# A transformer kernel on one core: score masks and norm scales moved from one engine to another

## The reference

```
for l in range(4):                                   # H = 16 heads of width 16
    h = rmsnorm(x, n1[l])
    q, k, v = split(h @ Wqkv[l].T + bqkv[l], 3)
    q, k = apply_rope(q), apply_rope(k)
    x = x + merge(sdpa(q, k, v, causal_bias)) @ Wo[l].T + bo[l]
    h2 = rmsnorm(x, n2[l])
    qc = h2 @ Wq_c[l].T
    kc, vc = split(memory @ Wkv_c[l].T, 2)
    x = x + merge(sdpa(qc, kc, vc, cross_bias)) @ Wo_c[l].T
    h3 = rmsnorm(x, n3[l])
    x = x + silu(h3 @ Wg[l].T) * (h3 @ Wu[l].T) @ Wd[l].T
# rmsnorm(x, w) = x * rsqrt(mean(x*x, -1) + eps) * w
# sdpa: softmax(q @ k.T * scale + bias) @ v; a bias is 0 where a key is allowed and -1e30 elsewhere
```

## Time and profile before

| what | value |
|---|---|
| median of 3 runs | 621.46 us (620.04 to 621.73) |
| span of the profiled execution | 617.9 us |
| TensorE busy | 564.1 us (91%) |
| weight loads busy (beside TensorE) | 421.8 us (68%) |
| VectorE busy | 353.5 us (57%) |
| ScalarE busy | 279.5 us (45%) |
| GpSimd busy | 117.7 us (19%) |
| instructions | 13676 |

### The profile page before, as it was taken

One profiled execution on the slowest core, in us unless ns is written; L12 is line 12 of the kernel. 1 busy time (PEld: TensorE's weight loads), 2 busy tenths in 40 slices (PEclk: granted clock), 3 DMA queues, 4 the chain that ended last, 5 costly groups with the idle time before them and its releaser, 6 DMA issues.

```text
span 617.9 us, 13676 instructions
## 1 busy us (share of the span) xinstructions
PE 564.1 (91%) x5806; PEld 421.8 (68%) x5806; DVE 353.5 (57%) x680; ACT 279.5 (45%) x490; POOL 117.7 (19%) x124
## 2 busy tenths in 40 slices
PE   4989998999999899999998989999898989999855
PEld 1666655988767566988766658987666558897523
DVE  5896445466564454674554455574554364752787
ACT  0254444633355336433544446342554547445523
POOL 4252100012323100020612000122312001252110
PEclk9999999999999999999999999999999999999969
DMA  8800020010500200201400200204000200000001
GB/s 334 345 2 25 12 69 2 5 65 1 205 2 4 102 1 3 68 1 27 180 1 36 70 2 2 69 1 189 16 2 1 71 0 2 0 1 2 2 1 39
DMA packets 4676, 30.29 MB, mean 49 GB/s; under 512 B 1153, under 2 KB 1665, under 8 KB 2818
## 3 DMA queue, kind: packets, MB, share of 16 engines
q1 hardware_dynamic: 4610, 29.35, 12.5%
HBM read 28.82 MB, written 0.52 MB: 47 GB/s over the span
## 4 chain that ended last, share of the span: by engine, by line
PE 77%; DVE 10%; ACT 8%; issue 3%; POOL 1%; DMA 1%; SPq 0%; DVEq 0%; POOLq 0%
PE psD L326 18%; PE QD L621 12%; PE psD L634 9%; PE QD L408 6%; PE QD L443 4%; ACT PTR L1253 3%; PE psD L320 3%; PE QD L436 3%; PE QD L394 3%; DVE AQ L1803 3%; PE psD L463 2%; PE QD L431 2%; PE psD L359 2%; PE psD L484 2%; PE psD L470 2%
## 5 line engine op out<-in xcount | busy, mean ns | idle before, releaser
L1253 ACT ACTIVATE PTR<-QD 128x2048 f32<-128x2048 f32 x40 | 75.1, 1878 | 41.8 <-PE QD L443 21.5
L326 PE MATMUL psD<-WAB,hT 128*128 128x256 f32 (+1 forms) x216 | 70.1, 465 | 2.2 <-DVE hT L1744 2.2
L2492 POOL TENSOR_TENSOR rstd<-ms,mhalf 128x2 f32<-128x2 f32 x26 | 19.9, 764 | 271.8 <-DVE ms L1729 270.6
L1803 DVE TENSOR_REDUCE AQ<-QD 128x8 f32<-128x2048 f32 (+1 forms) x24 | 55.0, 2290 | 27.0 <-PE QD L408 27.0
L621 PE MATMUL QD<-HH,WFH 128*128 128x256 f32 x224 | 67.4, 301 | 0.4 <-DVE WFL L1903 0.4
L1903 DVE TENSOR_TENSOR WFL<-WC,WFH 128x512 fp32r<-128x512 f32 x64 | 48.0, 755 | 32.2 <-ACT WFH L1297 32.1
L621 PE MATMUL QD<-HL,WFH 128*128 128x256 f32 x224 | 63.3, 283 | 0.0
L621 PE MATMUL QD<-HH,WFL 128*128 128x256 f32 x224 | 63.3, 283 | 0.0
L1800 DVE TENSOR_REDUCE AQ<-QD 128x16 f32<-128x2048 f32 x16 | 36.7, 2293 | 39.9 <-PE QD L408 39.9
L634 PE MATMUL psD<-WC,HID 128*128 128x256 f32 x256 | 58.2, 380 | 0.0
L326 PEld LDWEIGHTS psD<-WAB,hT 128*128 128x128 f32 x216 | 39.7, 195 | 21.0 <-issue 14.2
(11 more groups left out here) (172 smaller groups left out, 1021.2 us busy)
## 6 DMA issues: line engine op xcount, KB each, us to landing
WC<-in_wc SPq DMA_DIRECT2D x4, 3072.0 KB, 10.9
WAB<-in_wa SPq DMA_DIRECT2D x4, 1024.0 KB, 4.9
WAB<-in_wb SPq DMA_DIRECT2D x4, 1024.0 KB, 4.7
WF<-in_wf SPq DMA_DIRECT2D x1, 3072.0 KB, 22.8
bias<-in_bias SPq DMA_DIRECT2D x4, 512.0 KB, 3.4
WAB<-in_wt SPq DMA_DIRECT2D x1, 1024.0 KB, 6.0
X<-in_x SPq DMA_DIRECT2D x2, 256.0 KB, 2.8
out_x<-X SPq DMA_DIRECT2D x4, 128.0 KB, 2.4
```

The costliest lines, as they stand in the source:

```text
L326: mm = pe.matmul(bank(l, use)[:, col:col + n], lhs(k), rhs(k), start=(k == 0), stop=(k == KT - 1))
L1253: nc.scalar.activation(PTR[:, r % 2, :], QD[:, :], ACT.Exp, scale=SCALE).then_inc(t_exp, 1)
L1803: v = dve.tensor_reduce(QKR[b][:, t, 0, h, MAXROW].rearrange("p (s r) -> p r s", r=SG_H), QD[:, :].rearrange("p (r s n) -> p r s n", r=4, ...
```

## The change

Three things, and an order to go with them.

Scores: `scores` no longer writes the masks, and its matmuls start the bank afresh. `maxima` goes through the banks head by head: one `tensor_tensor_reduce` each, which multiplies nothing, adds the mask to the scores in place (`ALU.add`, scaled by -1) and keeps the running minimum, which goes to the head's own column of `MAXROW`. `causB` is now 256 wide, 0 in its left half and the causal mask in its right half. `QD` is read and written in place by these instructions.

Norms 0 and 1: `norm_T` transposes `X` itself and waits only for the residual; the scale rstd is multiplied in behind the projections, in `biased_qk`, `biased_v` and `cross_q`, where each row has its own partition again. `normalise` is left for i = 2 only. `add_bo` on GpSimd, which changes X, now waits until the transposes and the squares have read it.

Orders: the lists of calls of all engines are written in another order throughout.

```diff
@@ norm_T
-                pe.wait_ge(h_set[b], l * NORMS + i + 1)
-                transposes(l, f"n{i}{b}", hs[:, 2 * b:2 * b + 2, :])
+                if i == 2:
+                    pe.wait_ge(h_set[b], l + 1)
+                elif i == 1:
+                    pe.wait_ge(*emptied(l, f"wo{b}"))
+                elif l == 0:
+                    pe.wait_ge(x_set[b], 1)
+                else:
+                    pe.wait_ge(*emptied(l - 1, f"y{b}"))
+                transposes(l, f"n{i}{b}", (hs if i == 2 else X)[:, 2 * b:2 * b + 2, :])
@@ scores
-                    pe.wait_ge(mask_set, 1)
...
-                for a in range(4):
-                    if cross:
-                        pe.matmul(quad[a].rearrange("p (s n) -> p s n", s=2), identB[:, :],
-                                  maskB[:, 2 * b:2 * b + 2, :].rearrange("p t n -> p (t n)").unsqueeze(1).broadcast_to([P, 2, L]),
-                                  start=True, stop=False, skip_group_check=True)
...
-                                           QKT[b][rows(a), s, L:L + keys], start=False, stop=True, skip_group_check=True)
+                                           QKT[b][rows(a), s, L:L + keys], start=(at == 0), stop=True, skip_group_check=True)
@@ biased_qk
-                dve.tensor_tensor(QK[b][:, t, :], bank(l, use)[:, :], bias[:, 0:2 * D], ALU.add).then_inc(free(l, use), 1)
+                dve.scalar_tensor_tensor(QK[b][:, t, :], bank(l, use)[:, :], rstd[:, b, t:t + 1], bias[:, 0:2 * D], ALU.mult, ALU.add)\
+                   .then_inc(free(l, use), 1)
@@ maxima
                 if cross:
-                    v = dve.tensor_reduce(QKR[b][:, :, 0, h, MAXROW].rearrange("p t (s r) -> p r s t", r=SG_H),
-                                          QD[:, :].rearrange("p (r s t n) -> p r s t n", r=4, s=2, t=QT), AX_X, ALU.max, negate=True)
+                    if l == 0:
+                        dve.wait_ge(mask_set, 1)
+                    for a in range(4):
+                        for n, s in enumerate(ss):
+                            for q in range(QT):
+                                v = dve.tensor_tensor_reduce(quad[a][:, (2 * n + q) * P:(2 * n + q + 1) * P],
+                                                             quad[a][:, (2 * n + q) * P:(2 * n + q + 1) * P], maskB[:, 2 * b + q, :],
+                                                             -1.0, NO_MAX, ALU.add, ALU.min,
+                                                             accum_out=QKR[b][:, q, 0, SG_H * s + a, MAXROW:MAXROW + 1])
                 else:
-                    v = dve.tensor_reduce(QKR[b][:, t, 0, h, MAXROW].rearrange("p (s r) -> p r s", r=SG_H),
-                                          QD[:, :].rearrange("p (r s n) -> p r s n", r=4, s=len(ss)), AX_X, ALU.max, negate=True)
+                    keys = (t + 1) * P
+                    for a in range(4):
+                        for n, s in enumerate(ss):
+                            v = dve.tensor_tensor_reduce(quad[a][:, n * keys:(n + 1) * keys], quad[a][:, n * keys:(n + 1) * keys], causB[:, L - keys:L],
+                                                         -1.0, NO_MAX, ALU.add, ALU.min,
+                                                         accum_out=QKR[b][:, t, 0, SG_H * s + a, MAXROW:MAXROW + 1])
@@ cross_q
+                dve.wait_ge(rstd_set[b], l * NORMS + 2)
+                for t in range(QT):
+                    v = dve.tensor_scalar(QKR[b][:, t, 0, :, 0:HD], bank(l, use)[:, t * D:(t + 1) * D].rearrange("p (h d) -> p h d", h=H),
+                                          rstd[:, B + b, t:t + 1], None, ALU.mult)
@@ layer, TensorE (two of many lines)
+                scores(l, 8)
+                cross_qT(l, 1, 1)
                 outputs_T(l, 6)
-                scores(l, 8)
```

More of the change, by code:

```diff
@@ L922, in _ @@
             cross_kv(0, 0)
+            norm_T(0, 1, 0)
             pv(0, 3)
             scores_T(0, 4)
+            cross_kT(0, 0)
             maxima_T(0, 5)
+            cross_q(0, 0)
+            scores_T(0, 5)
+            cross_qT(0, 0, 0)
+            cross_qT(0, 0, 1)
             outputs_T(0, 3)
-            norm_T(0, 1, 0)
-            cross_kT(0, 0)
-            scores_T(0, 5)
-            cross_q(0, 0)
             pv(0, 4)
-            cross_qT(0, 0, 0)
+            scores(0, 6)
             outputs_T(0, 4)
-            cross_qT(0, 0, 1)
-            scores(0, 6)
             pv(0, 5)
@@ L1069, in rest @@
                 cross_kT(NL - 1, 1)
+                cross_qT(NL - 1, 1, 0)
                 pv(NL - 1, 6)
-                cross_qT(NL - 1, 1, 0)
+                scores(NL - 1, 8)
                 outputs_T(NL - 1, 6)
-                scores(NL - 1, 8)
                 pv(NL - 1, 7)
@@ L1112, in rest @@
                 gate_up(NL - 1, 1, 5)
+                down(NL - 1, 1, range(0, 4))
                 gate_up(NL - 1, 1, 6)
                 gate_up(NL - 1, 1, 7)
-                down(NL - 1, 1, range(0, 4))
                 window_T(0)
@@ L1839, in cross_q @@
                 no_maxima(b)
-                dve.tensor_copy(QKR[b][:, :, 0, :, 0:HD], bank(l, use)[:, :].rearrange("p (t h d) -> p t h d", t=QT, h=H))\
-                   .then_inc(free(l, use), 1)
+                dve.wait_ge(rstd_set[b], l * NORMS + 2)
+                for t in range(QT):
+                    v = dve.tensor_scalar(QKR[b][:, t, 0, :, 0:HD], bank(l, use)[:, t * D:(t + 1) * D].rearrange("p (h d) -> p h d", h=H),
+                                          rstd[:, B + b, t:t + 1], None, ALU.mult)
+                v.then_inc(free(l, use), 1)
             def cross_kv(l, b):
@@ L2089, in layer @@
                 residual(l - 1, 1, "y1")
+                biased_v(l, 0)
+                weigh_T(l, 0, 1)
                 mean_square(l, 0, 1)
-                normalise(l, 0, 1)
-                weigh_T(l, 0, 1)
-                biased_v(l, 0)
                 maxima(l, 2)
@@ L2106, in layer @@
                 maxima(l, 4)
+                cross_kv(l, 0)
                 residual(l, 0, "wo0")
-                cross_kv(l, 0)
+                maxima(l, 5)
+                split_low(l, 0)
+                weigh_T(l, 1, 0)
                 mean_square(l, 1, 0)
-                maxima(l, 5)
-                normalise(l, 1, 0)
-                weigh_T(l, 1, 0)
+                cross_q(l, 0)
                 divide(l, 3)
-                cross_q(l, 0)
                 maxima(l, 6)
@@ L2232, in _ @@
             maxima(0, 4)
+            mask_by_key()
             residual(0, 0, "wo0")
+            maxima(0, 5)
             mean_square(0, 1, 0)
-            maxima(0, 5)
-            normalise(0, 1, 0)
             cross_kv(0, 0)
@@ L2242, in rest @@
                 weigh_T(0, 1, 0)
+                cross_q(0, 0)
                 divide(0, 3)
-                cross_q(0, 0)
+                maxima(0, 6)
                 divide(0, 4)
-                maxima(0, 6)
                 divide(0, 5)
@@ L2251, in rest @@
                 split_low(0, 0)
+                split_low(0, 1)
+                weigh_T(0, 1, 1)
                 mean_square(0, 1, 1)
-                normalise(0, 1, 1)
-                weigh_T(0, 1, 1)
                 cross_q(0, 1)
-                split_low(0, 1)
+                maxima(0, 8)
                 divide(0, 6)
-                maxima(0, 8)
                 divide(0, 7)
@@ L2325, in rest @@
                 residual(NL - 2, 1, "y1")
+                biased_v(NL - 1, 0)
+                weigh_T(NL - 1, 0, 1)
                 mean_square(NL - 1, 0, 1)
-                normalise(NL - 1, 0, 1)
-                weigh_T(NL - 1, 0, 1)
-                biased_v(NL - 1, 0)
                 maxima(NL - 1, 2)
```

562 lines of the change are left out of this document (276 added, 286 removed).

## The result

The changed kernel takes 631.77 us (median of 4 runs, 630.66 to 632.27), the kernel before 620.75 beside it: ratio 1.0174 [1.0159, 1.019], so 11 us slower. I had forecast slower, which it is, but by 30.5 us. The profiled execution has a span of 630.5 us, 12.6 more than before.

What follows compares the result with a forecast made beforehand. TensorE, busy 96% of a layer, was taken as the bound, with a chain through QD's one set of banks hidden. Sum: 617.9 - 31.4 + 62 + 4 - 4 = 648.5 us span, so 652 us; range 603 to 703.

Steps and rivals of the forecast that it cites:

- masks off TensorE: By-query scores: removing their mask matmuls saves 7.9 us a layer, 31.4 us in all, without cover.
- norms, and the orders: Norms 0 and 1: transposes of X no longer wait for the normalised rows, and the start gets shorter: -4 us.
- maxima by masked pairs, with the queue on VectorE: Longer maxima stick out 15.6 us a layer, +62 us; VectorE work queued behind them adds +4.
- the cover of a round: Time from a reduce's start to TensorE's next use of QD, new order included: 2.25 to 4.25 us, 31 a layer.
- I take 0.25 + 0.07 = 0.32 and 0.38 + 0.07 = 0.45: VectorE's price in us of a pair over 128 and 256 columns, 0.07 for writing the result; maxima last 5.1 or 3.6.
- The stretch of gate_up and the quantised stage at the end stay as they are: End of the program: a sign of being right, that these parts do not change.
- the same 3.6 outside it: The median of the runs, 621.46 us, lies 3.6 us above the profiled span; added to the predicted span.
- C: Rival on the maxima: pair price just at the crossing, TensorE's waits equal its savings, 620 to 623 us; chance 0.06.
- the crossing: Pair price below which the change gains: about 0.27 and 0.40 us, where 8 us a layer stick out.
- A: Rival on the maxima: cheap pairs, 0.19 and 0.34 us, nearly all covered, 593 us; chance 0.18 for 593 to 619.
- B: Rival on the maxima: pairs at full cost, 0.48 and 0.61 us, 36 us a layer stick out, 735 us; chance 0.14.
- the waits on QD: Sign in TensorE's wait list: maxima of QD on top with some 60 us, in 30 or more places.

Runs made afterwards that it cites:

- o_plain: The kernel before, its orders and norms kept, with one reduce per round over scores that carry no mask: 593.46 us, 0.9553.
- n_plain: The changed kernel with one reduce per round over scores that carry no mask, new orders and norms kept: 596.42 us, 0.9609.
- o_masks: The kernel before with only the score masks moved to VectorE's pairs, norms and orders as before: 641.53 us, 1.0347.
- n_slow: The changed kernel with an unused 0.8 us VectorE reduce over constants ahead of every maximum: 661.9 us, 1.0639.
- n_cross: The changed kernel with self rounds masked on TensorE and one reduce each, only cross rounds masked by VectorE: 627.93 us, 1.0125.
- o_norms: The kernel before with only the two norms' scale moved behind the projections, masks and orders as before: 620.9 us, 1.0001.
- t_old: The changed kernel with before's order on four engines from the middle of the last layer's second feed-forward half to the end: 622.76 us, 1.005.
- n_warm: The changed kernel with dummy transposes on TensorE where it would wait ahead of the scores or the maxima's transposes: 632.33 us, 1.0191.

## Why the prediction was right or wrong

The 631.8 us lie inside the wide range of 603 to 703, and just below the forecast's own 634 to 684; the loss is a third of what was forecast. The spans 617.9 (before), 591.2 (o_plain), 594.6 (n_plain) and 630.5 (after) give each term of my sum its measured size:

| term | forecast | measured |
|---|---|---|
| masks off TensorE | -31.4 | -26.7 |
| norms, and the orders | -4 | +3.4 |
| maxima by masked pairs, with the queue on VectorE | +62 + 4 | +35.9 |
| sum | +30.6 | +12.6 |

**The maxima: right mechanism, wrong price.** This is the term that failed. The claim that the maxima on the one set of QD's banks become the wait, and that the cover of a round is 2.3 to 4.3 us, holds: o_masks, n_plain and n_slow show it. The step at fault is "I take 0.25 + 0.07 = 0.32 and 0.38 + 0.07 = 0.45". The first part was right to the hundredth, with some luck: the operations last 327 and 458 ns and not 291 and 424, but they overlap by 0.08 us and not by the 0.04 that I took from L1744 in the earlier trace rows, whose instructions come in twos, so that the 0.44 us are the mean of 0.40 and 0.48. The 0.07 us for the accumulator's result was not there: the read runs beside the next pair. The earlier trace rows had shown this on ScalarE (the next activation starts before the read ends), and I added 0.07 all the same. With 0.25 and 0.38, 4.25 and 3.35 us are needed, and against the same ten covers 0, 0, 0.35, 0.75, 0.75, 1.1, 1.45, 1.25, 1.45 and 1.25 us stick out: 8.4 us a layer, for which n_plain against after shows 7.7, 8.8 and 8.2. An error of 0.07 us in the pair was one of 7 us in a layer, because behind the cover every nanosecond of a pair counts 16 or 8 times a round.

The Trainium skill's 120 + columns cycles ("VectorE: DVE Perf Modes", section on the TRN2 errata), which I had put aside because the durations in the earlier trace rows were longer, give an estimate of 0.26 and 0.39 us, and the pairs follow each other at 0.25 and 0.38. In this trace the figure fits the pitch (start of one to start of the next), and not the duration of 327 and 458 ns. That an operation which writes out its accumulator is two instructions, as the same page of the Trainium skill says ("Two Vector instructions with no wait between them"), is what this trace shows; I had read it as speaking against the change, and the second instruction shows no cost here.

**Layer 0.** There 12.1 us stick out, not 8.4. I had scaled a steady layer by four. n_cross shows that it is the self rounds. That VectorE has the feeding work of the first layer to do at the start, which puts its longer maxima on the path, fits its 36.58 us of 46 but was not tested; up to 1.25 us are the lower clock's.

**The masks' removal** brought 7.2 us a steady layer for my 7.9, and 6.4 up to the first mark (100.68 for 107.04). Together with 1.3 us that o_plain loses in the tail this makes the 4.7 us of the table. Why a layer gives 0.7 us less stays open.

**The norms** brought 0.1 us or nothing (o_norms), not 4. In its trace the 11.9 us of L1735's waits have become 7.6 us on the X of the first layer norm, once, at the start, and 3.3 us in four places on what is left of L1735: the start had been waiting for X nearly as long, and the other waits were those of the third norm, which the edit leaves alone.

**The orders** I used only to correct the covers. "The stretch of gate_up and the quantised stage at the end stay as they are" was wrong by 7 to 9 us: t_old gives them back. I had compared the two orders where the edit was, and not at the end, where a reader of both lists could see that rounded_T(1) now stands ahead of hidden_T(0). With the price of a pair corrected, my sum is 617.9 - 31.4 + 33.6 + 4 - 4 = 620.1 us of span (624 with the same 3.6 outside it), and 630.5 was measured. The 10.4 us between are 7.4 for norms and orders (the tail's loss less what the orders gain in the layers), 4.7 for the masks' removal, and -1.7 for the pairs. With the tail's old order the change is nearly even (t_old, 1.005).

**The rivals.** C (the price just at the crossing) came nearest. I had put the crossing at 0.27 and 0.40 us a pair, which is a slip: with my own covers 9.7 us a layer stick out there, and the 8 us of the crossing belong to a little under 0.26 and 0.39, beside the measured pitch. The steady layers of the changed kernel are indeed at -0.75, +1.4 and -3.0 us against before. By the wrong crossing A's condition (a pair below 0.27) was met, but its time, 593 us, was that of a pair at 0.19. That o_plain, with no pairs at all, reaches 593.46 has nothing to do with A. B is out. Of the signs I named, the pitch was to tell ("wrong: a pair at 0.27 us or less"), and it did; the waits on QD are 27.7 us for 60, the layer 132 to 134 us for 140.

## What to carry to other kernels

Price a run of small instructions by its pitch (the start of one to the start of the next; busy time over count gives it only where many follow in a row), not by the duration of one: a result that is written behind can lie wholly beside the next. When an engine's work moves to one with idle time, ask what shares the resource between them: here the 7.2 us saved on TensorE in a steady layer came back as 7.7 to 8.8 us behind the same banks, and the gain was in having neither, since a maximum in a softmax needs no mask (as long as masked scores do not exceed the others by so much that the exponentials vanish; these runs use one input). And compare the orders of all engines to the program's end, since a new order may cost most where the edit is not.

## What the runs showed of the hardware

VectorE's read of its accumulator (512 in this run) lasts 0.14 us and starts with the next pair's main instruction. No delay by it is seen: pairs over 256 columns follow each other at 0.38 us, and this engine's operations over 256 columns of PSUM without an accumulator at 0.40 (L1744, from the 21.0 us that 48 of 480 ns fill in twos). No run has the same operation without its accumulator. The two-operand operation with an accumulator from PSUM lasts 327 ns over 128 columns and 458 over 256, and another follows after 0.25 and 0.38 us.

Some of VectorE's operations on SBUF got longer in the new orders, with or without the masks edit (927 and 883 ns in n_plain, 711 and 722 in o_norms for the same two). From the changed kernel:

```profile
L1791 DVE TENSOR_TENSOR AQ<-AQ,HID 128x512 f32<-128x512 f32 x16 | 14.8, 924 | 4.3 <-POOL HID L2521 4.0 <-DVE HID L1780 0.2
L1770 DVE TENSOR_TENSOR AQ<-HID,const 128x512 f32<-128x512 f32 x16 | 14.1, 882 | 0.2
...
L1730 DVE TENSOR_SCALAR hs<-X,rstd 128x256 f32<-128x256 f32 x16 | 8.4, 564 | 5.0 <-POOL rstd L2495 5.0
```

The last was 349 ns in the earlier trace rows; its mean rose by the one pair at 533.84 shown above. Two of L1950 took 2.38 us together from 567.72, while GpSimd's L2566 ran from 567.67 for 1.97 us, and they take 0.41 us each before. t_old, where no such scaling lies beside GpSimd's operations, has the short ones again; but it changes the orders of four engines at once, so that GpSimd is the cause is likely, not shown.

Ahead of the tail the lower clock came in one piece of 10.2 us in layer 0, where TensorE was busy 11.05 of 16 us and waited for maxima, and in three of 3.4 us in layers 1 and 2. In the first the 32 matmuls of a by-key score took 2.09 us for 1.17. With TensorE kept busy (n_warm, 13.27 of the 16 us) the granted clock was 1.00 there.
